# A fused attention and feed-forward kernel: feed-forward weight pieces moved out of the opening, the opening reordered, unread products placed in TensorE's waits

## What is computed

```python
q  = layernorm(x) @ Wq.T
k, v = split(ctx @ Wkv_expand.T)                    # 16 heads of 32
attn = softmax(where(causal, q k^T / sqrt(32), min))
x1 = x + tanh(g_xattn) * (attn v) @ Wout.T
gate, up = split(ste(layernorm(x1)) @ ste(w_gate_up).T)
out = x1 + tanh(g_ffn) * ste(silu(gate) * up) @ ste(w_down).T
```

## Time and profile before

| | |
|---|---|
| median of 3 runs | 743.07 us (741.93 to 746.26) |
| the profiled execution | 743.81 us, its span 742.0 us |
| PE busy | 705.7 us, 95% of the span |
| DVE / POOL / ACT busy | 608.5 (82%) / 570.9 (77%) / 418.4 us (56%) |
| granted TensorE clock, mean | 0.989 |

### The profile page before, as it was taken

One profiled execution on the slowest core, in us unless ns is written; L12 is line 12 of the kernel. 1 busy time (PEld: TensorE's weight loads), 2 busy tenths in 40 slices (PEclk: granted clock), 3 DMA queues, 4 the chain that ended last, 5 costly groups with the idle time before them and its releaser, 6 DMA issues.

```text
span 742.0 us, 17026 instructions
## 1 busy us (share of the span) xinstructions
PE 705.7 (95%) x5335; PEld 510.3 (69%) x5360; DVE 608.5 (82%) x1900; ACT 418.4 (56%) x658; POOL 570.9 (77%) x763
## 2 busy tenths in 40 slices
PE   3979999999999999999999998999999999999995
PEld 2868888889878888888888886565444444444442
DVE  5576878888888887787788887769999999999994
ACT  5457658668567567577576565265444344343441
POOL 6438768787787787787787877469888988888883
PEclk9989999999999999999999999999999999999998
DMA  8795977877886887877778759934566675565656
GB/s 250 186 247 158 253 159 220 238 178 210 219 209 192 231 199 210 208 212 211 190 217 226 189 139 236 271 102 121 87 163 143 145 165 132 144 154 129 159 124 193
DMA packets 137983, 137.59 MB, mean 185 GB/s; under 512 B 90381, under 2 KB 99879, under 8 KB 137767
## 3 DMA queue, kind: packets, MB, share of 16 engines
q1 hardware_dynamic: 136832, 135.97, 72.4%
q10 hardware_dynamic: 1063, 0.54, 0.4%
HBM read 40.24 MB, written 25.31 MB: 88 GB/s over the span
## 4 chain that ended last, share of the span: by engine, by line
PE 86%; DVE 4%; SPq 3%; DMA 3%; issue 2%; ACT 2%; POOL 1%; ACTq 1%; DVEq 0%; POOLq 0%
PE psum L2036 19%; PE psum L1642 12%; PE psum L1666 11%; PE psum L1708 10%; PE psum L2046 9%; PE psum L1595 5%; PE psum L1682 5%; PE psum L1654 3%; PE psum L1593 3%; PE psum L1629 3%; SPq L271 2%; PE psum L1684 2%; PE psum L1579 2%; DVE hmax L1503 1%; DMA heads<-nmT 1%
## 5 line engine op out<-in xcount | busy, mean ns | idle before, releaser
L1226 DVE CUSTOM_DVE_ANT_0 junk<-psum,mask 128x128 f32<-128x128 f32 (+1 forms) x512 | 152.3, 353 | 42.2 <-PE psum L1595 41.6
L2036 PE MATMUL psum<-w1q,xqb 128*128 128x512 bf16 (+1 forms) x753 | 158.3, 363 | 1.1 <-issue 0.3
L615 POOL TENSOR_SCALAR_AFFINE_SELECT prob<-prob 128x512 f32<-128x512 f32 x128 | 85.3, 666 | 71.1 <-ACT prob L924 69.7
L924 ACT ACTIVATE prob<-psum 128x768 f32<-128x768 f32 x128 | 103.7, 810 | 60.9 <-PE psum L1684 58.8
L798 POOL TENSOR_TENSOR hidden<-hidden 128x512 f32<-128x512 f32 (+1 forms) x94 | 110.8, 1194 | 29.4 <-ACT hidden L1141 29.3
L2036 PEld LDWEIGHTS psum<-w1q,xqb 128*128 128x128 bf16 x768 | 74.3, 98 | 80.2 <-issue 3.0
L1146 ACT ACTIVATE hidden<-hidden,round_bias,hinv 128x1408 f32<-128x1408 f32 x31 | 48.4, 1560 | 103.4 <-DVE hinv L1513 103.4
L623 POOL TENSOR_TENSOR prob<-prob 128x256 f32<-128x256 f32 x128 | 94.3, 743 | 6.2
L2046 PE MATMUL psum<-w2q,hqT 128*128 128x512 bf16 x331 | 79.0, 386 | 6.0 <-DMA hqT<-hq 5.4
L1642 PE MATMUL psum<-xT_hi,wq_hi 128*128 128x256 f32 x256 | 75.7, 296 | 0.5 <-POOL xT_lo L630 0.4
L1595 PE MATMUL psum<-heads 96*128 96x256 f32 x256 | 75.1, 335 | 0.0
(11 more groups left out here) (127 smaller groups left out, 1780.7 us busy)
## 6 DMA issues: line engine op xcount, KB each, us to landing
heads<-k_hi SPq DMA_DIRECT2D x128, 128.0 KB, 3.9
heads<-q_hi SPq DMA_DIRECT2D x128, 128.0 KB, 4.2
xln<-x_dram SPq DMA_DIRECT2D x16, 512.0 KB, 4.6
heads<-k_lo SPq DMA_DIRECT2D x64, 128.0 KB, 4.3
heads<-q_lo SPq DMA_DIRECT2D x64, 128.0 KB, 2.8
x<-x_dram SPq DMA_DIRECT2D x16, 512.0 KB, 4.6
x_scratch<-x SPq DMA_DIRECT2D x16, 512.0 KB, 4.8
x1b<-x_scratch SPq DMA_DIRECT2D x32, 256.0 KB, 3.4
```

Of the source, the lines that this page charges most:

```text
L615: pool.affine_select(out=blk, in_=blk, compare_op=ALU.is_ge, fill=0.0, base=0, pattern=[[0, 4], [1, P]], channel_multiplier=-1).then_inc(s ...
L924: act.activation(prob[:, g % 2, pair % 2, 0:CAUSAL // P].rearrange("p k h q -> p h k q"), psum[:, 2:4, 0:CAUSAL].rearrange("p h (k q) -> p ...
L1226: dve.tensor_tensor_reduce(junk[:, n % 2, 0:w], psum[:, h % 2, cols], m, 1.0, LOWEST, ALU.add, ALU.max, mx[:, X % 2, t, h:h + 1]).then_inc ...
L2036: last = pe.matmul(psum[:, bank, 0:w], xqb[:, t % 4, k, :], w1q[:, k, half * I + o:half * I + o + w], start=(k == 0), stop=(k == KH - 1))
```

## The change

Three things are changed. **Weights:** the opening rounds no piece (it only loads piece 0); slot b does `last_piece(b)`, and slots 2, 5 and 8 do two pieces, b = 2 the pieces 1 and 2, b = 5 the pieces 5 and 6, b = 8 the pieces 9 and 10. The second of the two is loaded in the slot itself. **Opening:** new lists on all engines; `ones(0)` goes behind `negate(0)`, `rsqrt1(0)` ahead of `split_context(0)` and `tables`, `low_weights(2)` ahead of the maxima, and DVE's first `low_weights` waits for `rs1`. **Unread products:** `spare` is called for 31 products instead of 15; 5 products stand in the ending ahead of the last batch's first `score_pair`, and 5 and 15 in the closing ahead of the last two whole `down`. Nothing of what is computed changes.

```diff
@@ -204,6 +204,15 @@
         def is_piece(i):
             return 0 <= i < PIECES
 
+
+        DOUBLE = (2, 5, 8)
+
+        def first_piece(b):
+            return b - 1 + sum(d < b for d in DOUBLE)
+
+        def last_piece(b):
+            return first_piece(b) + (b in DOUBLE)
+
         def of_w2(i):
 
             return i < KH
...
@@ -389,69 +398,64 @@
                 def opening():
                     load_context(1)
                     load_rows(1)
-                    load_weights(0)
                     spread_k_hi(0, 0)
                     spread_k_hi(0, 1)
                     spread_k_lo(0, 0)
                     spread_k_hi(0, 2)
                     spread_k_lo(0, 1)
+                    spread_k_lo(0, 2)
                     spread_q_hi(0, 0)
                     spread_q_lo(0, 0)
...
                     load_context(2)
-                    spread_k_lo(0, 3)
-                    load_weights(1)
-                    move_weights(0)
                     spread_q_hi(1, 0)
...
                     spread_k_hi(1, 3)
-                    move_weights(1)
-                    load_weights(2)
+                    spread_k_hi(2, 0)
                     spread_q_lo(2, 0)
+                    spread_q_hi(2, 0)
+                    load_weights(0)
+                    spread_q_lo(2, 1)
+                    spread_q_hi(2, 1)
...
-                    load_weights(3)
 
...
                 def slot(b):
...
-                    move_weights(b + 1)
+                    move_weights(last_piece(b - 1))
...
@@ -466,10 +470,13 @@
                     spread_k_lo(b + 2, 1)
                     spread_q_hi(b + 2, 2)
                     spread_q_hi(b + 2, 3)
+                    if b in DOUBLE:
+                        load_weights(last_piece(b))
+                        move_weights(first_piece(b))
                     spread_k_hi(b + 2, 1)
                     spread_q_lo(b + 2, 3)
                     spread_k_hi(b + 2, 2)
-                    load_weights(b + 3)
+                    load_weights(last_piece(b) + 1)
...
@@ -649,10 +656,9 @@
                                            ALU.mult, ALU.add).then_inc(s["xq_done"], 1)
 
                 def opening():
+                    rsqrt1(0)
+                    split_context(0)
                     tables()
-                    split_context(0)
-                    rsqrt1(0)
-                    spread_table()
...
+                    if b in DOUBLE:
+                        weights(first_piece(b))
...
-                    weights(b + 2)
+                    weights(last_piece(b))
...
                     high_k(0, 1)
                     copy_k(0, 0)
                     copy_k(0, 1)
+                    copy_v(0, 0)
+                    high_weights("wo", wo_hi, wo_raw, GROUPS)
+                    copy_v(0, 1)
                     high_q(0, 0)
-                    high_weights("wo", wo_hi, wo_raw, GROUPS)
                     high_q(0, 1)
...
+                    if b in DOUBLE:
+                        weights(first_piece(b))
...
-                    weights(b + 2)
+                    weights(last_piece(b))
...
@@ -1173,6 +1178,9 @@
 
                 def low_weights(n, hi, lo, raw):
                     dve.wait_ge(s["high"], n + 1)
+                    if n == 0:
+
+                        dve.wait_ge(s["rs1"], 1)
                     dve.tensor_tensor(lo[:], raw, hi[:].bitcast(F32), ALU.subtract).then_inc(s["split"], 1)
...
@@ -1304,39 +1312,37 @@
                         dve.reciprocal(winv[:, 0:n], kept).then_inc(s["w_inv"], 1)
 
                 def opening():
-                    ones(0)
                     measure_x(0)
                     low_weights(0, wkv_hi, wkv_lo, wkv_raw)
                     low_weights(1, wq_hi, wq_lo, wq_raw)
                     measure_x(1)
                     split_q(0, 0)
                     split_q(0, 1)
+                    low_weights(2, wo_hi, wo_lo, wo_raw)
+                    for h in range(0, 4):
+                        maxima(0, h)
                     spread_rows()
-                    weigh_rows(0)
-                    for h in range(0, 6):
-                        maxima(0, h)
+                    maxima(0, 4)
                     measure_x(2)
+                    maxima(0, 5)
                     split_q(1, 0)
                     maxima(0, 6)
                     split_q(1, 1)
                     for h in range(7, 16):
                         maxima(0, h)
                     negate(0)
-                    weigh_rows(1)
-                    low_weights(2, wo_hi, wo_lo, wo_raw)
-                    for h in range(0, 3):
-                        maxima(1, h)
+                    ones(0)
+                    maxima(1, 0)
+                    maxima(1, 1)
                     measure_x(3)
-                    for h in range(3, 8):
+                    for h in range(2, 5):
...
                     negate(1)
                     ones(1)
-                    weigh_rows(2)
                     reciprocals(0)
                     split_reciprocals(0)
...
@@ -1353,6 +1359,8 @@
                     maxima(b + 1, 4)
                     maxima(b + 1, 5)
                     split_q(b + 2, 1)
+                    if b in DOUBLE:
+                        weigh_rows(first_piece(b))
                     for h in range(6, 10):
                         maxima(b + 1, h)
                     step(b - 2, 0)
@@ -1365,8 +1373,8 @@
                     maxima(b + 1, 14)
                     maxima(b + 1, 15)
                     negate(b + 1)
-                    weigh_rows(b + 2)
-                    if b + 2 == PIECES - 1:
+                    weigh_rows(last_piece(b))
+                    if last_piece(b) == PIECES - 1:
                         dve.tensor_scalar(w_scale[:, W1T:NW], w_scale[:, W1T:NW], gates[:, 1:2], None,
                                           ALU.mult).then_inc(s["gate_step"], 1)
                     residual(b - 1, 0)
...
@@ -1671,10 +1680,14 @@
                 def score_pair(X, pair):
                     if not present(X):
                         return
+                    wait_for(pe, s["exp_done"], PAIRS * X + pair)
+                    if X == B - 1 and pair == 0:
+
+                        for i in range(5):
+                            pe.matmul(psum[:, 2, :], wo_hi[:, i % KH, 0:P], wo_hi[:, i % KH, :], start=True, stop=True)
                     if pair == 0:
                         pe.wait_ge(s["m_moved"], 2 * DMA * (X + 1))
                         pe.wait_ge(s["ones_set"], min(X + 1, 2))
-                    wait_for(pe, s["exp_done"], PAIRS * X + pair)
                     K = 3 * HD + 2
                     for d in range(2):
                         h, bank = 2 * pair + d, 2 + d
@@ -1713,8 +1726,8 @@
 
                 def spare(bank, n):
 
-                    if bank == 4:
-                        pe.wait_ge(s["v_copied"], 2)
+                    if bank == 2:
+                        pe.wait_ge(s["k_copied"], 1)
...
@@ -1746,80 +1760,87 @@
                     scores(0, 3)
                     queries(1, 1)
                     scores(0, 4)
...
+                    spare(2, 3)
...
                     scores(0, 15)
                     pe.wait_ge(s["t_copied"], 5)
                     transposed(2, 1)
+                    spare(2, 3)
                     maxima_rows(0)
                     pe.wait_ge(s["t_copied"], 6)
                     values(1, 0)
                     pe.wait_ge(s["k_copied"], 3)
                     queries(2, 0)
+                    spare(2, 6)
...
@@ -2059,10 +2080,20 @@
                     wait_for(pe, f["y_done"], t - 4)
                     down(t - 3)
 
+                def spare_down(n):
+
+                    pe.wait_ge(f["a_done"], 3 * LAST + 1)
+                    for i in range(n):
+                        pe.matmul(psum[:, 0, :], w2q[:, 0, 0:P], w2q[:, i % IT, :], start=True, stop=True)
+
                 def closing():
                     gates_and_ups(LAST)
                     for t in range(LAST - 3, LAST):
                         pe.wait_ge(f["y_done"], t - 1)
+                        if t == LAST - 2:
+                            spare_down(5)
+                        if t == LAST - 1:
+                            spare_down(15)
                         down(t)
                     pe.wait_ge(f["y_done"], LAST - 1)
```

More of the change, by code:

```diff
@@ L662, in opening @@
                     low_t(1, 1)
-                    weights(0)
+                    spread_table()
                     split_context(1)
@@ L979, in opening @@
                     copy_t(1, 1)
-                    weights(0)
                     high_q(1, 0)
                     high_q(1, 1)
-                    copy_v(0, 0)
-                    gate_values()
+                    norm1(2, 0)
                     high_k(1, 0)
@@ L987, in opening @@
                     high_k(1, 1)
-                    norm1(2, 0)
                     copy_k(1, 1)
@@ L996, in opening @@
                     move_rows(0)
```

(35 more changed lines are left out.)

112 lines of the change are left out of this document (53 added, 59 removed).

## The result

The changed kernel takes 773.51 us (median of 4 runs, 769.99 to 781.75) where the kernel before took 743.05 beside it: ratio 1.0388, 95% interval 1.0354 to 1.0421 (the ratio leaves out the longest run, 1.5% above the shortest). It is slower, as predicted, but by 30.5 us instead of 11.5, and 10.5 us outside the range.

A forecast was written before the change was run, and what follows sets the result against it. PE was taken to bound every slot. From the profiled 743.8 us, 7.5 (opening and start), 1.5 (ending) and 1.6 (closing) off and 22.1 (double slots) on gave 755.3; median forecast 754.6 us, 8-in-10 range 744 to 763.

The forecast's parts named there:

- the double slots' 22.1 us: Slots 2, 5 and 8: first piece, second piece and clock cost 8.3, 6.9 and 6.9 us, together 22.1 us more.
- The start: Kernel's first microseconds: memset off DVE's front saves 0.8 us, POOL's copy no longer slowed 1.0, together 1.8 us.
- The memset behind the negation: Opening, behind batch 0's negation: PE waits there for the moved k, not DVE, so the memset costs nothing.
- The rest of the opening: Up to slot 1: moved k lands 4.8 us sooner, 2.7 us from idle and clock; 7.5 us in total including the 1.8.
- The first piece: Double slots: one more weighing ahead of head 6's maximum makes PE lose 1.5 us in slot 2, 1.1 in 5 and 8.
- The second piece: the landing: Double slots: load lands in 5.0 us (5.6 in slot 2), so PE waits 4.3 us for the residual (5.3 in slot 2).
- The clock: Double slots: half clock behind PE's wait costs 1.5 us in each, bounds 0 and 1.7.
- The ending's 1.5: Before 479.17 us: five unread products fill a 1.7 us wait and keep the clock, gaining 1.5 us (0 to 1.7).
- the closing's 1.6: Last tiles: 15 unread products bring the clock to full, gaining 1.6 us (0 at half clock).
- rival of a longer landing: Double slots: a landing of 7.9 us adds 2.9, 2.9 and 2.3 us, giving 762.7 us; chance 0.14.

The follow-up runs named there:

- e1_no_doubles: The changed kernel with no slot taking two pieces, pieces 12 to 14 left out and only their stores made from copies: 740.93 us, 0.9957.
- e12_start_alone: The kernel before with only the start's change (memset off DVE's front, first low weights behind POOL's first deviation): 747.61 us, 1.0067.
- e7_heads_by_need: e2_load_early with the last sixteen transfers of SP's opening queue in order of need, low keys right behind the first high ones: 748.14 us, 1.0066.
- e15_need_no_doubles: e1_no_doubles with the opening queue of e7_heads_by_need, pieces 12 to 14 left out: 737.17 us, 0.992.
- e9_one_column: e7_heads_by_need with the scales of a two-column piece made by two 128x1 instructions instead of one of 128x2: 744.14 us, 1.0013.
- e13_rows_behind: The changed kernel with the next rows issued behind the second load and the store in slots 2, 5 and 8: 771.71 us, 1.0371.
- e2_load_early: The changed kernel with the second load and first piece's store issued about 4.3 us sooner in slots 2, 5 and 8: 750.69 us, 1.0093.
- e3_weigh_late: The changed kernel with the second weighing behind both residuals and measures on DVE in slots 2, 5 and 8: 761.23 us, 1.0217.
- e4_both: The changed kernel with the edits of e2_load_early and e3_weigh_late together: 751.65 us, 1.0093.
- e5_store_late: The changed kernel with the first piece's store issued behind the last spread of the high keys in slots 2, 5 and 8: 779.3 us, 1.0484.
- e10_behind_ten: e7_heads_by_need with a double slot's first piece weighed behind the tenth head's maxima instead of ahead of the seventh: 745.38 us, 1.0016.

## Why the prediction was right, and where it failed

The direction and the chain of waits were right; three terms of the sum were not. The experiments split the 18.9 us between 754.6 and 773.51 in two. Without the double slots' 22.1 us my sum gives 732.5, and `e1_no_doubles` took 740.93: 8.4 us, the opening (7.5 taken, 0.5 left by slot 2) and the ends. The double slots took 32.6 us for 22.1: 10.5 us, a landing taken too short and half clocks taken too short.

**The start** was right: 1.9 us by the first wait, for 1.8. Of the two operations that the same semaphore releases, POOL's began first and neither took visibly longer (DVE's subtraction had 1.23 before), so nothing came back on this chain:

```profile
7.41 0.19 POOL L590 TENSOR_TENSOR nb<-nb,rs 128x2 f32<-128x2 f32 x1
7.44 1.24 DVE L1184 TENSOR_TENSOR wkv_lo<-prob,wkv_hi 128x1024 fp32r<-128x1024 f32 x1 [1.45 <-POOL rs L588]
7.57 1.37 POOL L596 TENSOR_SCALAR c_hi<-craw 128x256 fp32r<-128x256 f32 x1
```

The cost seems to have fallen on POOL's next operation instead, the high part of the context: it ran beside the rest of that subtraction and took 1.37 us, for 0.41 before. PE's waits show no loss by it.

The memset behind the negation cost nothing, as I had it, but on a condition: that weighing and subtraction leave that place (`e12_start_alone`, 4.6 us of wait where they stay).

**The rest of the opening** failed at its end, and it is the largest single miss, 7.0 us. I gave 7.5 us for opening and start; slot 1's products begin 5.7 sooner, and nothing of my sum looked behind them. I had counted what leaves SP's queue ahead of the moved k, and not that SP, first come first served, stands 11.1 us at high keys which aren't made yet, so that the third batch's low keys go out 11 us after they are done. Slot 1 paid 3.5 us of wait and 3.4 us at half clock. With that mended 4.9 (`e7_heads_by_need`) to 5.9 us (`e15_need_no_doubles`) stay.

**The first piece** was 0.95, 1.60 and 1.62 us of wait for my 1.5, 1.1 and 1.1: near in the sum. What I missed is the 1.20 us of the scale's instruction beside POOL. The Trainium skill, "SBUF — State Buffer", section "Who interferes with whom", says that `tensor_scalar` can enter a mode with two ports, in which whichever of it and a GpSimd instruction issues first keeps the other out until it is done. The rows agree: beside a subtraction of POOL that had begun first, two columns took 1.20 us in `e7_heads_by_need` and two single ones 0.22 together in `e9_one_column`. I had used the same section for the start and not asked it here.

**The second piece: the landing.** "I take 5.0, nearest in place" is the step that failed here, worth 5.4 us of wait in the three slots. Measured were 7.3, 7.0 and 6.1 us; the waits were 7.07, 6.64 and 5.64 for my 5.3, 4.3 and 4.3. The 5.0 was the landing of moves that come ahead of the load, and the new load comes behind them and behind 512 KB of rows; in `e13_rows_behind` it lands in 4.4 to 6.0. The upper bound, 7.9, held. (Two readings were off by little: the 4.3 to 7.9 us of the opening are loads of 704 KB, not 512, and their median is 5.5, not 5.6.) The order "load, weigh, residual, queries" is shown by `e2_load_early` and `e3_weigh_late`: cut at either end, the wait goes. The Trainium skill, "DMA: Bandwidth & Descriptors", section "Anatomy of one DMA", gives its fit for transfers issued by GpSimd, and SP issues these. Its 3.2 us was never reached for 512 KB: the shortest second load took 4.1.

**The clock** was sized at 1.5 us a slot, 4.5 in all. The three slots lost 34.7 us, their six waits are 23.5, so 11.2 is left. Nearly all of it is half clock, as PE's time at 1.2 GHz behind these waits shows (columns as in the earlier trace rows):

```profile
142.00:148.00 6.00, 6.00 (x38) 4.38 (x39) 4.10 (x7) 0.87 (x1) 2.61 (x5) 0.50 0.00 1
220.00:226.50 6.50, 6.50 (x26) 5.70 (x30) 4.15 (x25) 3.53 (x8) 2.72 (x3) 0.50 0.40 102
242.40:247.00 4.60, 4.60 (x32) 3.46 (x36) 2.74 (x6) 0.83 (x2) 1.99 (x5) 0.50 0.00 2
338.40:342.60 4.20, 4.20 (x28) 3.29 (x32) 2.33 (x6) 0.83 (x2) 1.59 (x5) 0.50 0.02 4
```

That is 21.3 us at half clock, 10.7 lost. I took one stretch of 3.5 us per wait from the earlier trace rows; behind waits of 7.1, 6.6 and 5.6 us the stretches were 10.2, 6.8 and 6.8 us, each begun while PE still waited. Slot 5 had a second one behind 1.60 us of wait at its first weighing; slot 8 had none behind 1.62.

**The late places.** The ending's 1.5 came as 1.6 us (23.35 for 24.98) and the closing's 1.6 as 1.0. The ending's is not safe: in `e9_one_column` PE waited 1.66 us behind the five products, and the stage took 24.99. One stage earlier this execution took 32.6 us for 26.6, with 17.1 us at half clock; `e4_both` shows the same, `e2_load_early` (27.0) and `e9_one_column` (27.7) don't. What sets it off stays open.

**The sum** for the profiled execution: 755.3, and 12.6 us more for the double slots (5.9 of wait, 6.7 of clock), 7.0 for the opening, 6.0 for the last batch's clock and about 1 for the rest make 781.9; it took 781.75. The median, without the last batch's 6.0, is 754.6 + 12.6 + 7.0 = 774.2 by the same terms, for 773.51. My rival of a longer landing stood at 762.7, since it raised only the waits. A range that lets landing, clock and give-back go wrong together would have had to reach past 770.

## What to carry over

Where a bound engine has no slack, a transfer's cost is set by its place in the issuing queue: here the same two transfers, put ahead of six others, were worth 22.8 us. Price a new load also by the bytes that are issued just ahead of it, and give every new wait of PE the clock it loses behind it: here 10.2 us at half clock with the wait of 7.1 us, 6.8 with those of 5.6 and 6.6. And when an opening gets faster, follow each queue one stage further: what was done in time for the old pace is the next wait.

## What was not expected of the hardware

One VectorE instruction of 128x2 took 1.20 us, and ended with a GpSimd subtraction of 128x512 beside it; the same on 128x1 took 0.15 beside the same subtraction. The half clock does not need a long wait, and does not always follow one: with 1.6 us of idle time PE ran 3.4 to 6.8 us at 1.2 GHz in slot 5 of the changed kernel, of `e2_load_early` and of `e7_heads_by_need`, and stayed at the full clock in slot 8 of the changed kernel and in slots 5 and 8 of `e5_store_late`. In `e10_behind_ten` a wait of 0.83 us was followed by 3.4 us of it. And the mean clock of one kernel differs between executions, 0.967 to 0.984 for the changed one, and 0.991 to 1.00 for `e9_one_column`; there the executions spread over 741.9 to 748.6 us, the slowest at 0.991.
